# Applying the edge types once to 16 groups of a narrow round, and adding the 16 results in a row

## The reference

```python
h = jax.nn.relu(node_features @ node_proj_w.T + node_proj_b)
for l in range(L):                                          # L = 2, T = 8 edge types
    trans = jnp.einsum('nh,tdh->tnd', h, edge_W[l])
    msgs = trans[edge_type, src]
    agg = jax.ops.segment_sum(msgs, dst, num_segments=num_nodes)
    h = jax.nn.relu(_gru_cell(agg, h, gru_wih[l], gru_whh[l], gru_bih[l], gru_bhh[l]))
return h @ out_w.T + out_b
```

## Time and profile before

| | |
|---|---|
| median of 3 timed runs | 1657.53 us (1656.12 to 1658.63) |
| span of the profiled execution | 2243.1 us |
| mean granted TensorE clock in it | 0.846 |
| PE matmul busy | 1624.5 us, 10492 instructions |
| PE weight loads busy (they overlap matmuls) | 1125.6 us |
| POOL busy | 1201.0 us |
| DVE busy | 751.5 us |
| ACT busy | 527.8 us |

### The profile page before, as it was taken

How to read it: one execution, slowest core, us unless ns; L and a number is a source line. 1 busy time by engine, 2 the same in 40 slices (tenths; PEclk the granted TensorE clock), 3 DMA queues, 4 the chain that set the end, 5 groups by cost and what they waited for, 6 DMA issues and landing times.

```text
span 2243.1 us, 34109 instructions
## 1 busy us (share of the span) xinstructions
PE 1624.5 (72%) x10492; PEld 1125.6 (50%) x10493; DVE 751.5 (34%) x3350; ACT 527.8 (24%) x1268; POOL 1201.0 (54%) x1282
## 2 busy tenths in 40 slices
PE   6468777786867755777775887778787775767776
PEld 4345444444544544556553544545454454555555
DVE  6544332423222243343334122212322223333433
ACT  5132232404233112222211111111413311122221
POOL 6455555555555554544453555555555555555552
PEclk9689898898889877877787899889888987788888
DMA  6324536262543322222222766664243253222221
GB/s 170 102 61 158 155 100 207 71 217 86 179 132 85 99 63 63 67 60 62 60 64 73 234 227 202 204 227 133 67 113 83 71 148 82 63 68 66 64 64 37
DMA packets 183315, 251.55 MB, mean 112 GB/s; under 512 B 24396, under 2 KB 156641, under 8 KB 183201
## 3 DMA queue, kind: packets, MB, share of 16 engines
q0 software_dynamic: 58176, 119.22, 19.3%
q1 hardware_dynamic: 123041, 130.73, 18.5%
q10 hardware_dynamic: 1984, 0.13, 0.1%
HBM read 211.87 MB, written 38.12 MB: 111 GB/s over the span
## 4 chain that ended last, share of the span: by engine, by line
another core or an unknown queue 35%; PE 33%; issue 11%; DVE 10%; ACT 4%; DVEq 3%; DMA 3%; POOL 1%; SPq 0%; ACTq 0%; POOLq 0%
PE ps L1042 9%; PE ps L1113 6%; PE ps L1019 6%; PE ps L1105 4%; PE ps L980 3%; DMA blocks<-node_table 2%; PE ps L1093 2%; DVE acc L1618 2%; DVE onehot L1541 1%; ACT counts L756 1%; DVE acc L1638 1%; ACT sums_sb L822 1%; DVEq L1611 1%; DVE onehot L1576 1%
## 5 line engine op out<-in xcount | busy, mean ns | idle before, releaser
L589 POOL DMA_INDIRECT gath<-node_table,gidx x1212 | 1165.0, 961 | 997.3 <-ACT gidx L627 532.5
L1042 PE MATMUL ps<-counts,blocks 128*128 128x504 f16 (+3 forms) x1764 | 426.1, 388 | 76.1 <-issue 49.6
L1638 DVE TENSOR_TENSOR acc<-ps,acc 128x16 f32 x864 | 151.1, 175 | 901.5 <-remote 364.6
L822 ACT COPY sums_sb<-ps 128x512 f32<-128x512 f32 x216 | 126.5, 586 | 922.9 <-remote 598.4
L1113 PE MATMUL ps<-sums_sb,wT 128*128 128x128 f32 x1728 | 262.1, 315 | 99.9 <-ACT sums_sb L822 81.8
L1019 PE MATMUL ps<-work 128*128 128x392 bf16 x983 | 224.7, 367 | 147.5 <-ACT counts L756 55.4
L1042 PEld LDWEIGHTS ps<-counts,blocks 128*128 128x128 bf16 x1764 | 173.0, 102 | 280.5 <-issue 102.0
L1113 PEld LDWEIGHTS ps<-sums_sb,wT 128*128 128x128 f32 x1728 | 249.7, 227 | 114.3 <-issue 65.5
L1105 PE MATMUL ps<-onehot,gath 128*128 128x128 bf16 x2592 | 204.3, 230 | 62.5 <-issue 37.7
L1093 PE MATMUL ps<-sums_sb,wT 128*128 128x96 f32 (+1 forms) x1408 | 212.9, 310 | 47.4 <-issue 29.7
L1093 PEld LDWEIGHTS ps<-sums_sb,wT 128*128 128x128 f32 x1408 | 202.8, 224 | 71.0 <-issue 57.2
(11 more groups left out here) (198 smaller groups left out, 867.4 us busy)
## 6 DMA issues: line engine op xcount, KB each, us to landing
blocks<-node_table SPq DMA_DIRECT2D x84, 672.0 KB
kept_counts<-counts SPq DMA_DIRECT2D x28, 882.0 KB
counts<-kept_counts SPq DMA_DIRECT2D x28, 882.0 KB
gath<-node_table,gidx POOLq DMA_INDIRECT x1212
node_table<-gath SPq DMA_DIRECT2D x14, 336.0 KB, 3.2
node_table<-work SPq DMA_DIRECT2D x14, 336.0 KB
counts<-in_x_dram SPq DMA_DIRECT2D x1, 3080.0 KB
out_dram<-counts SPq DMA_DIRECT2D x13, 224.0 KB
```

Of the source, the lines that this page charges most:

```text
L589: nc.gpsimd.indirect_dma_start(out=gath[:, b, j, :], out_offset=None, in_=tables[l], in_offset=bass.IndirectOffsetOnAxis(ap=gidx[:, b, j:j ...
L822: act.copy(n_sb[:, b // 2, b % 2 * BG:(b % 2 + 1) * BG, :], narrow_sums[b % 2]) \
L1042: last = nc.tensor.matmul(head_ps[:, 0:COLS[share]], blocks[:, j % 2, at, part * H:(part + 1) * H], counts[:, a, 0:COLS[share]], start=(i ...
L1638: nc.vector.tensor_tensor(win, narrow_ps[q][:, g * NARROW:(g + 1) * NARROW], win, ALU.add) \
```

## The change

Rounds with windows of 16 apply the types once to all 16 groups: `narrow_types(k)` issues eight matmuls with 256 columns behind the fourth slot's work and writes them to PSUM bank 4. Before that, half 0 had its call behind the third partial sums. The copied sums of a round lie in one buffer, of which ACT's first copy waits for the types of the round before. On DVE, the one-hots of the next round's slot b follow the partial sums of slot b; the adds of all 16 groups follow at the end of the round. The first list of head one-hots is made behind slot 0's one-hots; the second is spread over the 16 adds.

```diff
--- before.py
+++ after.py
@@ -285,7 +285,7 @@
         onehot = sb("onehot", [GE, SLOTS, BG, CODES], BF16)
         sums_sb = sb("sums_sb", [H, 2, 2 * BG * NCODES])
         s_sb = sums_sb[:, :, 0:BG * CODES].rearrange("p a (g c) -> p a g c", c=CODES)
-        n_sb = sums_sb.rearrange("p a (g c) -> p a g c", c=NCODES)
+        n_sb = sums_sb.rearrange("p a (g c) -> p (a g) c", c=NCODES)
 
         early = blocks.rearrange("p b a f -> p (b a f)").bitcast(F32)
         yT = early[:, 0:2 * TILE].rearrange("p (b c) -> p b c", b=2)
@@ -313,7 +313,7 @@
         sums = [ps[:, 2 * b:2 * b + 2, 0:2 * CODES].rearrange("p a (g c) -> p a g c", c=CODES) for b in range(2)]
         narrow_sums = [ps[:, 2 * b, :].rearrange("p (g c) -> p g c", c=NCODES) for b in range(2)]
         win_ps = [ps[:, 4 + b, 0:BG * WIN] for b in range(2)]
-        narrow_ps = [ps[:, 4 + q, 0:2 * BG * NARROW] for q in range(2)]
+        narrow_ps = ps[:, 4, 0:ROUND * NARROW]
         proj_ps = [ps[:, 2 + b, 0:TILE] for b in range(2)]
         rows_ps = [ps[0:ROWP, b, :].rearrange("p (c h) -> p c h", c=TC) for b in (4, 5, 0, 1)]
         yT_ps = [ps[:, 6 + b, 0:TILE] for b in range(2)]
@@ -818,8 +818,9 @@
                     k = n * SLOTS
                     for b in range(SLOTS):
                         act.wait_ge(es[l]["sums_ready"], k + (b + 1 + SLOTS))
-                        act.wait_ge(es[l]["win_done"], k + b // 2 * 2)
-                        act.copy(n_sb[:, b // 2, b % 2 * BG:(b % 2 + 1) * BG, :], narrow_sums[b % 2]) \
+                        if b == 0:
+                            act.wait_ge(es[l]["win_done"], k + 2)
+                        act.copy(n_sb[:, b * BG:(b + 1) * BG, :], narrow_sums[b % 2]) \
                            .then_inc(es[l]["sums_copied"], 1)
                         update(b, n, begin, tile, head)
 
@@ -1106,15 +1107,15 @@
                                                     onehot[:, b, j, 0:NCODES], start=(part == 0), stop=(part == PARTS - 1))
                     last.then_inc(es[l]["sums_ready"], 1)
 
-                def narrow_types(k, q):
-                    pe.wait_ge(es[l]["sums_copied"], k + (2 * q + 4))
-                    pe.wait_ge(es[l]["acc_added"], (k + 2 * q) * BG)
+                def narrow_types(k):
+                    pe.wait_ge(es[l]["sums_copied"], k + (SLOTS + 2))
+                    pe.wait_ge(es[l]["acc_added"], (k + 2) * BG)
                     for t in range(T):
-                        last = nc.tensor.matmul(narrow_ps[q].rearrange("p (g w) -> p g w", g=2 * BG),
+                        last = nc.tensor.matmul(narrow_ps.rearrange("p (g w) -> p g w", g=ROUND),
                                                 wT[:, W_EDGE + l * T + t, :],
-                                                n_sb[:, q, :, t * NARROW:(t + 1) * NARROW],
+                                                n_sb[:, :, t * NARROW:(t + 1) * NARROW],
                                                 start=(t == 0), stop=(t == T - 1))
-                    last.then_inc(es[l]["win_done"], 2)
+                    last.then_inc(es[l]["win_done"], SLOTS)
 
                 def gates_begin(k, i):
 
@@ -1137,15 +1138,13 @@
                     narrow_sums_of(k, landed, 2)
                     if head is None:
                         piece(pe, begin, gate_in, l + 1, tile)
-                    narrow_types(k, 0)
-                    if head is None:
                         piece(pe, begin, gate_z, l + 1, tile)
                     else:
                         head_slot(l, head + 2)
                     narrow_sums_of(k, landed, 3)
                     if head is not None:
                         head_slot(l, head + 3)
-                    narrow_types(k, 1)
+                    narrow_types(k)
                     if head is None:
                         piece(pe, begin, to_rows, l + 1, tile)
 
@@ -1618,47 +1617,47 @@
                         nc.vector.tensor_tensor(win, win_ps[b % 2][:, j * WIN:(j + 1) * WIN], win, ALU.add) \
                           .then_inc(sem_l["acc_added"], 1)
 
-                def add_narrow(k, g0, q, after_head, hots):
-                    if len(hots) <= FIRST_HOTS:
-                        for g in hots:
-                            make_hots(g)
-                        hots = []
-                    for half in range(2):
+                def add_narrow(k, g0, after_head, hots):
+                    dve.wait_ge(sem_l["win_done"], k + (SLOTS + 2))
+                    if after_head:
+                        dve.wait_ge(head_added, after_head)
+                    for b in range(SLOTS):
                         _, starts = nc.values_load_multi_w_load_instructions(
-                            start_row[0:1, ds(g0 + half * BG, BG)], engines=(mybir.EngineType.DVE,), min_val=0, max_val=N,
+                            start_row[0:1, ds(g0 + b * BG, BG)], engines=(mybir.EngineType.DVE,), min_val=0, max_val=N,
                             skip_runtime_bounds_check_because="start_row is clamped to N, and nodes are not negative")
-                        if half == 0:
-                            dve.wait_ge(sem_l["win_done"], k + (2 * q + 4))
-                            if after_head:
-                                dve.wait_ge(head_added, after_head)
                         for j in range(BG):
-                            g = half * BG + j
+                            g = b * BG + j
                             win = acc[:, ds(starts[j], NARROW)]
-                            dve.wait_ge(sem_l["acc_added"], k * BG + ((2 * q + 2) * BG + g))
-                            nc.vector.tensor_tensor(win, narrow_ps[q][:, g * NARROW:(g + 1) * NARROW], win, ALU.add) \
+                            dve.wait_ge(sem_l["acc_added"], k * BG + (2 * BG + g))
+                            nc.vector.tensor_tensor(win, narrow_ps[:, g * NARROW:(g + 1) * NARROW], win, ALU.add) \
                               .then_inc(sem_l["acc_added"], 1)
-                            for more in hots[g * len(hots) // (2 * BG):(g + 1) * len(hots) // (2 * BG)]:
+                            for more in hots[g * len(hots) // ROUND:(g + 1) * len(hots) // ROUND]:
                                 make_hots(more)
 
                 def narrow_round(n, head=None, last=False):
                     if head is None:
                         begin, tile = round_tile(dve, mybir.EngineType.DVE, n)
                     k = n * SLOTS
-                    for q in range(2):
-                        g0 = n * ROUND + 2 * q * BG
-                        if head is None and q == 0:
+                    hots = [MADE[l].get(head + 2 * q, []) if head is not None else [] for q in range(2)]
+                    for b in range(SLOTS):
+                        dve.wait_ge(sem_l["sums_ready"], k + (b + 1 + SLOTS))
+                        (one_hots if last else narrow_hots)(n * ROUND + (ROUND + b * BG), b)
+                        if head is not None:
+                            if b == 0:
+                                for g in hots[0]:
+                                    make_hots(g)
+                            if b < 2:
+                                head_slot(l, head + b, (k + 2) * BG)
+                        elif b == 1:
                             piece(dve, begin, before_tanh, l + 1, tile)
-                        hots = MADE[l].get(head + 2 * q, []) if head is not None else []
-                        add_narrow(k, g0, q, added_until(l, head + 2 * q) if head is not None else 0, hots)
-                        for b in (2 * q, 2 * q + 1):
-                            (one_hots if last else narrow_hots)(n * ROUND + (ROUND + b * BG), b)
-                        if head is not None:
-                            for b in (2 * q, 2 * q + 1):
-                                head_slot(l, head + b, (k + 2 * q + 4) * BG)
-                        elif q == 0:
+                        elif b == 2:
                             piece(dve, begin, new_state, l + 1, tile)
-                        else:
-                            piece(dve, begin, state_parts, l + 1, tile)
+                    add_narrow(k, n * ROUND, added_until(l, head + 2) if head is not None else 0, hots[1])
+                    if head is not None:
+                        for b in range(2, SLOTS):
+                            head_slot(l, head + b, (k + 2 + SLOTS) * BG)
+                    else:
+                        piece(dve, begin, state_parts, l + 1, tile)
 
                 def one_round(p, n):
                     begin, tile = round_tile(dve, mybir.EngineType.DVE, n)
```

## The result

The changed kernel takes 1658.20 us (median of 20 runs, 1648.6 to 1665.3), the kernel before 1651.24 us in the runs beside it (20 runs, 1646.7 to 1658.8). The ratio is 1.0033 with a 95% interval from 1.0017 to 1.0049: **slower by 0.33%**, 5.4 us, the difference of the averages (the medians lie 7.0 us apart). A second set of runs gave 1.0041 (1.0025 to 1.0058). I had forecast no change. The median after lies near the 1657.0 us of the forecast only because the three runs shown of before lay at 1657.5.

What follows compares the result with a forecast made beforehand. The gather queue was taken as the bound: 57.1 + 15.4 + 35.0 + 34.7 + 1212 x 1.25 = 1657.2 us against the median of 1657.5. Less 0.5 us from PE, the forecast was 1657.0 us, range 1647 to 1669.

Steps and rivals of the forecast that it cites:

- What bounds the kernel: Whole kernel: POOL's gather queue sets the pace, 1212 gathers 1.25 us apart, 20.0 us a round; chance 0.64.
- the 15.4: POOL's extra wait after the 16 gathers that need no sum: 15.72 us, 15.4 more than its usual 0.30.
- Mostly the profiled execution's own: Late PE results, 7 to 10 us after their recorded end, taken as mostly absent from timed runs; 586 us of span.
- Types on PE: Narrow rounds: one call of 256 columns replaces two of 128; gain 0 to 0.2 us a round, 0.1 taken.
- The rival in which PE sets the pace: Head rounds: PE is the bound, 48 rounds gain 0.1 us each, 1652.5 us; chance 0.18.
- DVE order: End of narrow rounds: 16 adds take 5.4 us, work behind them is late; 0 taken under the gather queue.
- a late second list: Rival: head one-hots behind the adds come up to 2 us late in 11 rounds, 1668.5 us; 0.18 with late adds.
- the prediction's last part: Expected profile of the changed kernel: longer PE waits for one-hots at L1019 would show the late list.
- the 58.4 us of the earlier trace: PE's wait for one-hots at L1019 in the kernel before, cited for the late-list rival.
- POOL and SP: Gather queue: no DMA issued or moved, order of waits kept, POOL's pitch stays 1.25 us.
- Gate pieces: `gates_begin` waits for all adds: PE up to 2.9 us longer in 8 rounds, 23 us at most; 0 taken.
- the 0.18 for slower: Chance of the slower case, late list or late adds before `gates_begin`: 1668.5 us, up to 1680.6.

Runs made afterwards that it cites:

- the account: Eight profiled executions of about 1650 us (two changed, one before, five variants): start-to-start gaps of POOL's gathers summed above 1.25 us, split into gather length and idle time.
- The kernel before with blocks: Kernel before with every list of head one-hots, up to the limit of 12, made in one block ahead of the adds: 1662.22 us, 1.0083.
- pauses: Changed kernel with a one-element DVE operation (135 ns) ahead of each of the 192 head one-hot pairs: 1653.60 us, 1.0033.
- the kernel before with pauses: Kernel before with a one-element DVE operation ahead of each of the 192 head one-hot pairs: 1641.64 us, 0.9966.

## Why the prediction was wrong

**What bounds the kernel.** The reading was right: the gather queue sets the pace. Its arithmetic was not. I wrote that 57.1 + 15.4 + 35.0 + 34.7 + 1515 = 1657.2 us met the median of 1657.5, and took the match as proof. The profile after has none of the 15.4, 24.3 in place of 35.3 at the layer break, 22.7 in place of 36.0 at the end, and 34.6 us spread over the other gathers, which I had set to zero. The match was luck: stalls of a 2205 us execution stood in for hold-ups of a 1650 us one. "Mostly the profiled execution's own" failed as well: whole sets of timed runs take 2205 us.

**Types on PE.** Right. The call was to take 3.47 to 3.57 us in its matmuls' spacing and about 3.7 us in full; the shortest of the 54 calls lasts 3.62 us, the one above 3.72. Two old calls of 1.95 us against one of 3.62 give back 0.28 us a round at most, 0.12 by spacing (the records of the new call start 0.216 us apart); that it buys no time at 1650 us, as said, fits POOL's pace and wasn't tested by itself. The rival in which PE sets the pace is out: the types' matmuls are busy 198.6 us, against 221.2 in the kernel before at 1640 us, and the kernel is longer; POOL idles only 1 to 8 us outside the layer break in all eight executions of the account.

**DVE order.** The adds take 5.9 us, not 5.4 (1.60 us from one four to the next). The price that I worked out, 0 to 2.1 us in 11 rounds for a late second list, was of the wrong thing, and the 0 that I took holds: making the list early again gained nothing (1.0054). PE's wait for one-hots did grow, as the prediction's last part said it would for a late list: the waits of the changed kernel have

```profile
PEld ps L1020 <- DVE work L1497: 35.7, 53, 2.8
```

against 21.3 us in the kernel before at 1640 us (the 58.4 us of the earlier trace rows are of a 2243 us execution). These 14 us were covered, as I had taken them to be: with the early list the wait is 23.2 us and the time no shorter.

**POOL and SP. This is the step that failed:** "No DMA is issued or moved." True, and I concluded that gathers cost what they cost before. They don't: what DVE runs beside them sets how long they last, and the change moved DVE's first lists of more than eight pairs from between adds into a block. Expected 0; in the two profiles the gathers last 9.0 and 11.0 us longer than in the kernel before, 8.3 and 5.8 us of it in rounds 10 to 14. The two kernels don't overlap in this: 15.8 to 20.8 us above 0.946 each in the four profiles of the kernel before, 29.8 and 31.8 in the two of the changed one. The kernel before with blocks shows the path from DVE's order to the time, at 0.83%. The trace of before had the sign: gathers of 961 ns on average where the undisturbed one lasts 946, 1212 times.

**Gate pieces.** "PE may wait 2.9 us longer ... POOL's 20 us cover it: 0 taken." At the end of the narrow rounds of layer 1 the wait was 4.1 us longer (5.43 against 1.37), and PE came out of it at the lower clock, 1.8 us more, a term that the sum doesn't have. The cover held in most of these rounds but not in that one, where POOL idled about 3 us more. The price was mis-sized and its cover taken for whole. I had given late adds a part of the 0.18 for slower; they are one part of the cause, the gathers were in no rival.

**What stays open.** The two places make up 11.0 us of the account's 12.9 in the first profile and 9.2 of 16.0 in the second; by the ratios the kernels differ by 5.4 and 6.8 us (the medians by 7.0 and 7.9). But removing one at a time didn't bring the time back: pauses took the gathers of rounds 10 to 14 from 10.5 to 6.6 us and the median by 0.7 us only, and halving the list, in whose profile both were smaller (9.2 and 0.1 us), left the ratio at 1.0037. With a spread of 10 us and more between executions and one profile for each, the share of each mechanism is not settled, and neither is why pauses help the kernel before by 0.34% though its one profile shows no less gather time (23.1 against 20.8). That version, the kernel before with pauses, is faster than both kernels.

## What to carry to other kernels

Where DMAs issued by GpSimd set the pace, an order on VectorE can be a cost of theirs: ahead of moving SBUF-to-SBUF operations together, look how long the DMA issues last under them. And an account of waits is good only for the sort of execution that it is read from: see that the profiled time is one of the timed ones before adding its stalls to a sum that should meet their median.

## What was unexpected of the hardware

**Hold-ups by blocks.** A gather of 0.95 us can last 4.45 us under ten unbroken one-hot pairs and 6.43 us under twelve, while five gathers under fourteen others lasted 1.03 us at most. An operation of one element (135 ns) between the pairs brings the longest from 4.45 to 2.25 us, but all gathers together only from 31.8 to 25.8 us above 0.946 each. The pairs are f16 to bf16 operations, most of them of 0.23 to 0.35 us each; twelve bf16 one-hots of L1575 in a row held nothing (0.95 us).

**Two times for one program.** The same kernel took 1645 to 1651 us in three sets of runs and 2203 to 2208 us in four others, and the runs of a set stayed together. The mean durations of DVE's adds and of ACT's and POOL's work are the same in both (adds 174 and 175 ns, sum copies 586 ns, gathers 963 and 959 ns). What differs is how soon ACT can start on PE's results: in the narrow rounds, where ACT had idled 0.25 us or more, its copy starts 0.04 us (median) after the recorded end of the partial sums, and 0.08 us on average, in the profile of the kernel before at 1642 us; in two profiles of it at 2187 and 2218 us the medians are 1.6 and 1.3 us, the means 2.5 and 2.3, and one in ten is over 5.7 us. POOL's waits for indices rise with it, from 21.9 us to this row of the kernel before at 2218 us:

```profile
L589 POOL DMA_INDIRECT gath<-node_table,gidx x1212 | 1162.4, 959 | 974.3 <-ACT gidx L627 538.1 <-issue 343.9 <-DMA node_table<-work 35.4
```

The mean granted clock is 0.85 to 0.86 there and 0.95 at 1650 us. Whether it is cause or consequence, and what makes the results late, no run here shows.
